# Two of every 64 tiles of both gather sums fetched row by row by SyncE and ScalarE, and copied into the ring by VectorE

## The chip, the core and the metric

The program runs on one NeuronCore of a Trainium2 chip. The metric is the device time of one execution in microseconds (us); lower is better. The core has five engines that run their own instruction streams and meet at semaphores: TensorE (PE), VectorE (DVE), ScalarE (ACT), GpSimd (POOL) and SyncE (SP). Sixteen DMA engines move data between device memory (HBM) and the on-chip memory (SBUF); SP, ACT and POOL can issue DMAs.

## What is computed

Four graph layers over 3,125 nodes of 128 numbers and 100,000 edges. Only the last layer touches the change. Cut to that:

```python
ht = jnp.einsum('ne,reh->rnh', hidden, weights[l])      # 18 transformed rows per node
msg_f = ht[edge_type, src] + biases[l][edge_type]
out = jax.ops.segment_sum(msg_f, dst, num_segments=n_nodes)
msg_b = ht[edge_type + n_rel, dst] + biases[l][edge_type + n_rel]
out = out + jax.ops.segment_sum(msg_b, src, num_segments=n_nodes)
```

So each edge picks one row of 128 numbers (512 bytes) from a table of 28,800 rows, and the rows are summed by node: once forward (table `y_forward`, edges sorted by `dst`) and once backward (table `y_back`, edges sorted by `src`).

## The kernel before

**Tiles, pairs and groups.** The 100,000 sorted edges are 782 tiles of 128 edges (`TILES`), the nodes 25 blocks of 128 (`BLOCKS`). A pair is a tile with a block that its edges fall in; there are 806 pairs. `gather_sum` (L928) works on groups of 8 pairs (`GROUP`), 101 groups in all. It is called twice: with the tag g3 for the forward sum (`back=True`, a straight program without a loop), then g4 for the backward sum (mostly a hardware loop over 8 groups).

**The four streams of a gather sum.** POOL issues one indirect DMA per tile (L1032), which fetches 128 rows into one of 64 slots of the ring `got` (8 groups; `RING` = 8). From tile group 8 on it first waits (L1029) until TensorE has finished group g-5, so it can be five groups ahead. DVE makes, for each group n, the 8 one-hot matrices `hot` in one instruction (`compare`, L1042), at the earliest when TensorE has finished group n-4, four buffers being there. TensorE (`landed_group`, L1124) loads 16 register values (8 column and 8 slot offsets), waits for `hot` and for the eight landings of the group, and multiplies 8 pairs into PSUM.

**What runs beside it in g3.** The table `y_back` for g4 is computed inside g3. Behind every group 15b/4 (rounded down) TensorE multiplies block b in three pieces (`rows_of`, L1139), each of which waits for DVE's bias addition of the piece before; DVE does `bias` for block b (L1046) when its loop is at the group after. The two buffers `y[:, 0]` and `y[:, 1]` are stored by SP (even b) and ACT (odd b) in `keep_rows` (L974), and `bias` of block b waits for the store of block b-2. Also in g3, the index tables of g4 are made: DVE's `climb` at group 3, a table turned by TensorE behind group 6, `locals_of` and `rows_named`, and seven pieces that TensorE flattens (`flatten`, L1148), six of them copied out of PSUM by ACT (L1008). In g4 SP and ACT have no work.

**Order.** All of this order is written by hand: by the place of each call in the loop over n.

Of the kernel before, what the change touches and what calls it, by code (L numbers as in the profile page):

```python
# [71 lines left out]
BANK = 512  # L72

# [854 lines left out]
def gather_sum(nc, S, dram, tag, name, table, index, fresh=True, back=False):  # L928
# [5 lines left out]
    WHOLE, REST = divmod(GROUPS, RING)  # L934
    with ExitStack() as stack:
        m = Memory(nc, stack)
        got = m.sb(tag + "_got", [P, SLOTS * D])
        hot = m.sb(tag + "_hot", [P, WAYS, GROUP, P])
# [6 lines left out]
        if back:  # L945
# [11 lines left out]
                                           "listed", "order", "packed", "built", "flat", "placed", "filed"))  # L957
            by_src = dram["rec_by_src"].rearrange("(t e) r -> t (e r)", e=P)
# [3 lines left out]
            CLIMB_AT, ROWS_AT, FLIP_AT, LOCAL_AT, NAMED_AT, ROWS_BEFORE = 3, 8, 6, 24, 30, 8  # L962
# [11 lines left out]
        def keep_rows(eng, k, first, last):  # L974
            for b in range(first + k, last, 2):
                eng.wait_ge(biased, (b + 1) * PIECES)
                eng.dma_start(dram["y_back"][b * P:(b + 1) * P, :], y[:, k, :]).then_inc(saved[k], 16)
            if last == BLOCKS:
                eng.wait_ge(saved[k], 16 * ((BLOCKS + 1 - k) // 2))

        @block.sync
        def _(sp):
            if back:
                even = TILES // 16 * 16
                sp.dma_start(firsts[0:1, 0:even].rearrange("o (a b) -> o a b", a=16),
                             by_src[0:even, 0:1].rearrange("(a b) o -> o a b", a=16), allow_slow_non_contiguous=True).then_inc(fetched, 16)
                sp.dma_start(firsts[0:1, even:TILES], by_src[even:TILES, 0:1].rearrange("a o -> o a"),
                             allow_slow_non_contiguous=True).then_inc(fetched, 16)
                sp.wait_ge(fetched, 32)
                sp.dma_start(dram["src_firsts"].rearrange("(a n) -> a n", a=1), firsts[:, :]).then_inc(stored, 16)  # L990
                sp.wait_ge(stored, 16)
                sp.dma_start(s.climb[:, :], dram["src_firsts"].rearrange("(a n) -> a n", a=1).to_broadcast([P, TILES])).then_inc(climbing, 16)
                keep_rows(sp, 0, 0, ROWS_BEFORE)
                sp.wait_ge(listed, 1)
                sp.dma_start(S["src_steps"][0:1, :].rearrange("o (c p) -> o c p", p=P), s.turned_columns[:, :]).then_inc(filed, 16)
                sp.wait_ge(built, 1)
                sp.dma_start(tile_rows[:, 0:full, :], by_src[0:full * P, :].rearrange("(c p) r -> p c r", p=P)).then_inc(carried, 16)
                sp.dma_start(tile_rows[0:rest, full, :], by_src[full * P:TILES, :]).then_inc(carried, 16)
                keep_rows(sp, 0, ROWS_BEFORE, BLOCKS)
                sp.wait_ge(filed, 16)  # L1000

        @block.scalar
        def _(act):
            if back:
                keep_rows(act, 1, 0, ROWS_BEFORE)
                for n, (array, k, lo, hi) in enumerate(flats):
                    act.wait_ge(flat, n + 1)
                    act.activation(array[:, lo:hi], free[:, 0:hi - lo], ACT.Copy).then_inc(placed, 1)  # L1008
                keep_rows(act, 1, ROWS_BEFORE, BLOCKS)
                act.wait_ge(placed, len(flats))  # L1010

        @block.gpsimd
        def _(pool):
# [6 lines left out]
            for g in range(TILE_GROUPS):  # L1020
# [10 lines left out]
                for c in range(g * GROUP, min((g + 1) * GROUP, TILES)):  # L1031
                    pool.indirect_dma_start(out=got[:, (c % SLOTS) * D:(c % SLOTS + 1) * D], out_offset=None, in_=table,  # L1032
# [3 lines left out]
        def _(dve):  # L1036
# [38 lines left out]

            def locals_of():
# [4 lines left out]
            def rows_named():  # L1081
# [6 lines left out]
                                         t[:, 0:full, :, 2], ALU.mult, ALU.add).then_inc(built, 1)  # L1088

            if back:  # L1090
                for n in range(GROUPS):
# [14 lines left out]
                dve.wait_ge(built, 2)  # L1106
                dve.wait_ge(listed, 1)
            else:
                with dve.Fori(0, WHOLE) as i:
                    for k in range(RING):  # L1110
                        dve.wait_ge(summed[k % WAYS], i * (RING // WAYS) + (k // WAYS + 1))
                        compare(k % WAYS, start_of(i, k))
# [5 lines left out]
        def _(pe):  # L1118
# [5 lines left out]
            def landed_group(i, k, lands, pairs=GROUP):  # L1124
# [4 lines left out]
                if lands:  # L1129
                    pe.wait_ge(landed[k], i * (16 * GROUP) + 16 * lands)  # L1130
# [914 lines left out]
def norm_and_messages(nc, S, dram):  # L2045
# [4 lines left out]
    with ExitStack() as stack:  # L2050
# [38 lines left out]
        def _(act):  # L2089
# [11 lines left out]
            for b in range(BLOCKS):  # L2101
# [4 lines left out]
                if b == FLAT_AT:  # L2106
                    act.wait_ge(flat, 1)
# [3 lines left out]
            act.wait_ge(placed, 1)  # L2111
# [93 lines left out]
def gnn_kernel(nc, ins, out):  # L2205
# [14 lines left out]
    with ExitStack() as stack:  # L2220
# [54 lines left out]
        with ExitStack() as last:  # L2275
# [3 lines left out]
            S["src_steps"] = r.sb("src_steps", [1, 3 * PAIR_COLS], I32)  # L2279
            with ExitStack() as third:  # L2280
# [5 lines left out]
                gather_sum(nc, S, dram, "g3", "dst", tables[0], S["d_msg"], back=True)  # L2286
            gather_sum(nc, S, dram, "g4", "src", tables[1], S["s_msg"], fresh=False)
# [25 lines left out]
```

## Time and profile before

| | |
|---|---|
| median of 3 runs | 5433.64 us (5424.72 to 5434.58) |
| the profiled execution | 5436.53 us, of which the span is 5434.8 us |
| POOL busy over the span | 3413.0 us (63%), 3213 instructions |
| PE busy over the span | 3062.4 us (56%) |
| g3, first to last indirect DMA | 3150.1 to 4278.8 us |
| g4, first to last indirect DMA | 4292.2 to 5397.8 us |
| TensorE's granted clock | 0.62 of full speed in g3, 0.57 in g4 |

The two gather sums take the span from 3150 to 5411 us, 42% of it; what follows is a short last normalisation. An instruction's row in a timeline gives its start, its duration, its engine, its line, what it writes and reads, how many like it were merged, and in brackets how long the engine was idle before it and which event ended that idle time. "issue" means that the engine waited for nothing that the profile shows. A group of instructions that share a line gives the number, and the shortest, median and longest duration in ns.

### The profile page before, as it was taken

The page shows a single profiled execution, that of the slowest core. Times are in us where ns is not written, and L with a number is a line of the kernel's source. Part 1 is how long each engine was busy: PE and PEld are TensorE (multiplying, and loading weights), DVE is VectorE, ACT ScalarE, POOL GpSimd, SP SyncE. Part 2 cuts the span into 40 slices and gives each one's busy share as a digit, 9 for nine tenths or more (in the row PEclk, how much of TensorE's full clock was granted, in tenths as well). Part 3 has the DMA queues.
Part 4 walks back from the last instruction along what each step waited for, and adds up shares of the span by engine and source line. Part 5 has one row for each costly group of instructions (what it writes and reads, how often), then busy time and mean ns, then how long its engine had stood idle before and what let it go on. Part 6 is the DMA issues. An engine that isn't in the chain of part 4 may idle for free. (4 is left out here: it accounts for less than half of the span.)

```text
span 5434.8 us, 50013 instructions
## 1 busy us (share of the span) xinstructions
PE 3062.4 (56%) x13750; PEld 2237.6 (41%) x13751; DVE 2231.2 (41%) x2709; ACT 614.3 (11%) x1076; POOL 3413.0 (63%) x3213
## 2 busy tenths in 40 slices
PE   3899989567777777744918633343333333333333
PEld 1788879233333333324917422232222323232223
DVE  7999985445555454568901331111111111101112
ACT  0455540000000000004701000000000000000000
POOL 2888868466556555657770356666666666666664
PEclk7999999666666666657958766665665656555555
DMA  5566667144444444425825332222222111111111
GB/s 177 157 181 192 177 198 230 37 131 138 132 133 139 132 135 130 139 87 159 259 62 195 136 100 70 69 64 60 60 59 60 48 46 46 45 46 46 46 46 46
DMA packets 498663, 599.91 MB, mean 110 GB/s; under 512 B 190115, under 2 KB 367441, under 8 KB 496248
## 3 DMA queue, kind: packets, MB, share of 16 engines
q0 software_dynamic: 117856, 246.12, 16.5%
q1 hardware_dynamic: 337751, 229.77, 14.8%
q10 hardware_dynamic: 42944, 122.68, 6.0%
q8 instruction: 51, 0.84, 0.1%
q14 instruction: 61, 0.49, 0.0%
HBM read 406.69 MB, written 204.36 MB: 112 GB/s over the span
## 5 line engine op out<-in xcount | busy, mean ns | idle before, releaser
L720 POOL DMA_INDIRECT rec_by_src<-rec,pos x782 | 1123.3, 1436 | 524.6 <-issue 238.9
L1132 PE MATMUL ps<-g_got,g_hot 128*128 x3224 | 687.5, 367 | 1225.8 <-issue 797.4
L1132 PEld LDWEIGHTS ps<-g_got,g_hot 128*128 128x128 f32 x3224 | 605.7, 272 | 1320.2 <-issue 1318.9
L1592 POOL DMA_INDIRECT sc_kv<-kv,d_src x806 | 761.8, 945 | 533.9 <-DVE sc_kve L1644 260.2
L1032 POOL DMA_INDIRECT g_got<-y_forward,d_msg x782 | 739.3, 945 | 381.8 <-issue 230.1
L1032 POOL DMA_INDIRECT g_got<-y_back,s_msg x782 | 737.8, 943 | 381.2 <-issue 233.5
L805 PE MATMUL ps<-ln_low,ln_hot 128*125 128x256 f32 x2848 | 620.3, 381 | 20.3 <-DVE ln_low L782 16.1
L805 PEld LDWEIGHTS ps<-ln_low,ln_hot 128*125 128x125 f32 x2848 | 535.6, 188 | 104.8 <-issue 24.4
L1043 DVE TENSOR_TENSOR g_hot<-ps,src_loc 128x1024 f32<-128x1024 f32 x101 | 120.6, 1221 | 992.5 <-remote 450.4
L1699 PE MATMUL ps<-w_e,sc_attrT 128*128 128x512 f32 x404 | 320.0, 887 | 246.0 <-ACT sc_attrT L1611 216.3
L1051 DVE TENSOR_TENSOR g_y<-ps,ms_b 128x384 f32<-128x384 f32 x75 | 41.8, 558 | 808.8 <-remote 474.2
L1695 PE MATMUL ps<-q,sc_hotT 128*128 x1616 | 308.5, 352 | 108.0 <-DVE sc_hotT L1637 92.0
L1644 DVE TENSOR_TENSOR sc_kve<-sc_kv,ps 128x1024 f32<-128x1024 f32 x202 | 244.9, 1212 | 239.2 <-DMA win_rows<-rec_by_dst,win_tilei 163.3
L1695 PEld LDWEIGHTS ps<-q,sc_hotT 128*128 128x128 f32 x1616 | 283.2, 262 | 130.2 <-issue 130.2
L1682 PE MATMUL ps<-sc_locr,ones 1*128 1x512 f32 x404 | 312.8, 864 | 10.4 <-issue 10.4
L1637 DVE TENSOR_SCALAR sc_hotT<-ps,part 128x512 f32<-128x512 f32 x202 | 148.0, 747 | 379.5 <-PE ps L1682 196.3
L1145 PE MATMUL ps<-ms_w,ms_xT 128*128 128x384 f32 x150 | 105.9, 800 | 250.0 <-DVE g_y L1051 166.0
L777 DVE TENSOR_TENSOR ln_low<-col,win_lo 128x1024 f32<-128x1024 f32 x178 | 219.7, 1234 | 4.9 <-PE ps L805 2.6
L782 DVE TENSOR_TENSOR ln_low<-ln_low,win_w 128x1024 f32<-128x1024 f32 x178 | 216.1, 1214 | 0.0
L779 DVE TENSOR_TENSOR ln_hot<-col,win_key 128x1000 f32<-128x1000 f32 x178 | 213.8, 1201 | 0.0
L2030 ACT ACTIVATE n_root<-n_var 128x25 f32<-128x25 f32 x1 | 0.2, 225 | 1812.2 <-DVE n_var L2019 1812.2
L828 ACT ACTIVATE ln_out<-ps 125x1024 f32<-125x1024 f32 x160 | 163.7, 1023 | 311.3 <-PE ps L805 294.5
(323 smaller groups left out, 3283.7 us busy)
## 6 DMA issues: line engine op xcount, KB each, us to landing
linked<-ln_out SPq DMA_DIRECT2D x320, 224.0 KB
ve<-sc_kve ACTq DMA_DIRECT2D x202, 256.0 KB
wv_ve<-ve SPq DMA_DIRECT2D x101, 512.0 KB
l_links<-linked SPq DMA_DIRECT2D x25, 800.0 KB
l_links<-linked ACTq DMA_DIRECT2D x25, 800.0 KB
f_links<-linked SPq DMA_DIRECT2D x25, 800.0 KB
f_links<-linked ACTq DMA_DIRECT2D x25, 800.0 KB
attr_pairs<-ln_feats POOLq DMA_DIRECT2D x7, 2048.0 KB
```

The lines of the kernel that those rows point to most:

```text
L720: pool.indirect_dma_start(out=dram["rec_by_src"], out_offset=bass.IndirectOffsetOnAxis(ap=S["pos"][:, c:c + 1], axis=0), in_=S["rec"][:, c ...
L777: dve.tensor_tensor(low[:, q, :, 0:P], S["col"][:, :].unsqueeze(1).to_broadcast([P, GROUP, P]), S["win_lo"][:, cols].unsqueeze(2).to_broad ...
L779: dve.tensor_tensor(hot[:, q], S["col"][:, 0:KEYS].unsqueeze(1).to_broadcast([P, GROUP, KEYS]), S["win_key"][:, cols].unsqueeze(2).to_broa ...
L782: dve.tensor_tensor(low[:, q, :, P:2 * P], low[:, q, :, 0:P], S["win_w"][:, cols].unsqueeze(2).to_broadcast([P, GROUP, P]), ALU.mult).then ...
L805: last = pe.matmul(ps[0:KEYS, bass.ds(slots[j], 2 * P)], hot[:, q, j, :], low[:, q, j, :], start=False, stop=True, skip_group_check=True)
L1032: pool.indirect_dma_start(out=got[:, (c % SLOTS) * D:(c % SLOTS + 1) * D], out_offset=None, in_=table, in_offset=bass.IndirectOffsetOnAxis ...
L1132: last = pe.matmul(ps[:, bass.ds(columns[j], width)], hot[:, q, j, :], got[:, bass.ds(slots[j], width)], start=False, stop=True, skip_grou ...
L1592: pool.indirect_dma_start(out=kv[:, q, j, :], out_offset=None, in_=dram["kv"], in_offset=bass.IndirectOffsetOnAxis(ap=S["d_src"][:, c:c + ...
L1644: dve.tensor_tensor(kve[:, q].rearrange("p a (k d) -> p k a d", d=D), kv[:, q].rearrange("p k (a d) -> p k a d", a=2), feat(q).rearrange(" ...
L1682: pe.matmul(spread_loc(q), S["ones"][0:1, :], locr[0:1, q, :], start=True, stop=True).then_inc(spread[q], 1)
L1695: pe.matmul(qe(q)[:, j * D:(j + 1) * D], hot_t[:, q, j * P:(j + 1) * P], S["q"][:, bass.ds(cols[j], D)], start=True, stop=True)
L1699: pe.matmul(feat(q), attr_t[:, q % 2, :], S["w_e"][:, :], start=True, stop=True).then_inc(product[q], 1)
```

## The change

In every ring of 64 tiles, two tiles are no longer fetched by POOL: the last tile of group 3 is fetched by ACT, the last tile of group 7 by SP (`HELPERS`). That holds for the first 12 rings (`WHOLE`), so for 24 of 782 tiles in each gather sum. A helper loads eight row numbers at a time into registers from a flat index table (`rows`, new: `d_rows` and `s_rows`), and issues one DMA of one row of 512 bytes for each; 128 of them make a tile. The row lands in a buffer of its own, `aside`, which holds two tiles per helper. DVE waits for 128 landings, copies the tile into its slot of the ring and raises `handed` (`hand`); TensorE waits for `handed` in that group beside seven landings instead of eight. A helper starts on tile k+2 when tile k was handed.

In g4 the helpers do only this (`rows_alone`). In g3 (`rows_and_tables`) the stores of `y_back` and SP's three table DMAs stand between quarters of a tile (32 rows). The six flattened pieces are copied by DVE (`place`) instead of ACT, `FLIP_AT` goes from 6 to 5, and `NAMED_AT` from 30 to 36.

```diff
+            def hand(e, h, count):
+                dve.wait_ge(fetched_rows[e][h], count)
+                dve.tensor_copy(got[:, at:at + D], aside[e][:, h * D:(h + 1) * D]).then_inc(handed[e], 1)
...
+    HELPERS = {"act": RING // 2 - 1, "sp": RING - 1}
+    QUARTER = P // 4
...
+        def fetch_rows(eng, e, kind, i, h, lo, hi):
+            p = tile_of(e, h)
+            for at in range(lo, hi, GROUP):
+                _, named = nc.values_load_multi_w_load_instructions(
+                    rows[p:p + 1, bass.ds(i * P + at, GROUP)], engines=[kind], min_val=0, max_val=ROWS * RELATIONS - 1,
...
+                for j in range(GROUP):
+                    eng.dma_start(aside[e][at + j:at + j + 1, h * D:(h + 1) * D],
+                                  table[bass.ds(named[j], 1), :]).then_inc(fetched_rows[e][h], 16)
+
+        def rows_and_tables(eng, e, kind, k):
+            stored = 0
+            for n in range(4 * WHOLE):
+                i, h = divmod(n // 4, 2)
+                while (stored * 2 + k < BLOCKS and (15 * (2 * stored + k)) // 8 + 2 <= n
+                       and (15 * (2 * stored + k)) // 4 + 1 < n // 4 * RING + HELPERS[e]):
+                    keep_rows(eng, k, 2 * stored + k)
+                    stored += 1
...
+                if n % 4 == 0 and n >= 8:
+                    eng.wait_ge(handed[e], n // 4 - 1)
+                fetch_rows(eng, e, kind, i, h, n % 4 * QUARTER, (n % 4 + 1) * QUARTER)
...
+        def rows_alone(eng, e, kind):
+            for h in range(2):
+                fetch_rows(eng, e, kind, 0, h, 0, P)
+            with eng.Fori(1, WHOLE // 2) as i:
+                for h in range(2):
+                    eng.wait_ge(handed[e], i * 2 + (h - 1))
+                    fetch_rows(eng, e, kind, i, h, 0, P)
...
                 for c in range(g * GROUP, min((g + 1) * GROUP, TILES)):
+                    if c in helped:
+                        continue
                     pool.indirect_dma_start(out=got[:, (c % SLOTS) * D:(c % SLOTS + 1) * D], out_offset=None, in_=table,
...
                     compare(q, n * GROUP)
                     if n - 1 in beside:
                         bias(beside[n - 1])
+                    for e in helper_of(n):
+                        k = n // RING
+                        hand(e, k % 2, (k // 2 + 1) * (16 * P))
+                    if n - 1 in flat_at:
+                        place(flat_at[n - 1])
                     if n == CLIMB_AT:
                         climb()
...
                 if lands:
-                    pe.wait_ge(landed[k], i * (16 * GROUP) + 16 * lands)
+                    own = k in HELPERS.values()
+                    pe.wait_ge(landed[k], i * (16 * (GROUP - own)) + 16 * (lands - own))
+                    for e in helper_of(k):
+                        pe.wait_ge(handed[e], i + 1)
```

**ACT in g3.** Before, its whole stream of g3 is six rows: the stores of blocks 1, 3, 5, 7, then the six copies out of PSUM, then the stores of the eight other odd blocks (`g_y` is `y`).

```order
L977 DMA y_back<-g_y 128x1152 x4
L1008 ACTIVATE src_loc<-ps 128x384 x2
L1008 ACTIVATE src_loc<-ps 128x128
L1008 ACTIVATE s_msg<-ps 128x384 x2
L1008 ACTIVATE s_msg<-ps 128x14
L977 DMA y_back<-g_y 128x1152 x8
```

Now the same engine, where it stores block 9, inside the tile for group 35 (L997 is a row's DMA with the register instruction in front of it, L993 the load of eight row numbers, L1032 the store):

```order
L997 ISA
L997 DMA g_aside_act<-y_forward 1x128
L1032 DMA y_back<-g_y 128x1152
L993 TENSOR_LOAD d_rows
L997 ISA
L997 DMA g_aside_act<-y_forward 1x128
```

The store, which waits for block 9's bias additions, now has the first two quarters of the tile ahead of it and the last two, 64 rows, behind it.

**DVE in g3.** Before, from the bias additions of block 9 on (L1051 `bias`, L1043 `compare`):

```order
L1051 TENSOR_TENSOR g_y<-ps,ms_b 128x384 x3
L1043 TENSOR_TENSOR g_hot<-ps,dst_loc 128x1024 x4
L1051 TENSOR_TENSOR g_y<-ps,ms_b 128x384 x3
```

Now, from the same additions on (L1099 `bias`, L1091 `compare`, L1127 `hand`):

```order
L1099 TENSOR_TENSOR g_y<-ps,ms_b 128x384 x3
L1091 TENSOR_TENSOR g_hot<-ps,dst_loc 128x1024
L1127 COPY g_got<-g_aside_act 128x128
L1091 TENSOR_TENSOR g_hot<-ps,dst_loc 128x1024
L1142 SCALAR_TENSOR_TENSOR rec<-src_rows 14x128
```

One compare behind the additions of block 9, DVE now waits for ACT's tile, with all later compares behind that wait.

## Rows read from the trace of the kernel before

**Rows 1.** The page: busy time of each engine.

```profile
PE 3062.4 (56%) x13750; PEld 2237.6 (41%) x13751; DVE 2231.2 (41%) x2709; ACT 614.3 (11%) x1076; POOL 3413.0 (63%) x3213
```

**Rows 2.** Stretches g3 and g4: bounds, length, busy PE PEld DVE ACT POOL, clock, DMA.

```profile
3150.00:4292.00 1142.00, 412.94 (x1777) 307.41 (x1777) 174.75 (x208) 2.42 (x6) 745.92 (x789) 0.62 0.22 62
4292.00:5411.00 1119.00, 376.78 (x1612) 332.63 (x1612) 120.59 (x101) 0.00 (x0) 737.75 (x782) 0.57 0.17 46
```

**Rows 3.** Line 1032: duration ns min/median/max, first and last start in us.

```profile
L1032 POOL DMA_INDIRECT g_got<-y_forward,d_msg x782: 938/944/2419, 3150.1 to 4278.8; - x196
L1032 POOL DMA_INDIRECT g_got<-y_back,s_msg x782: 938/944/961, 4292.2 to 5397.8; - x196
```

**Rows 4.** Timeline of POOL in g4, around one of its stops.

```profile
5363.67 0.94 POOL L1032 DMA_INDIRECT g_got<-y_back,s_msg  x1 [0.30 <-issue]
5364.92 0.94 POOL L1032 DMA_INDIRECT g_got<-y_back,s_msg  x1 [0.30 <-issue]
5371.55 0.94 POOL L1032 DMA_INDIRECT g_got<-y_back,s_msg  x1 [5.69 <-DMA alpha<-mx_turn]
```

**Rows 5.** Timeline of PE over the same stretch.

```profile
5334.77 2.29 PE L1132 MATMUL ps<-g_got,g_hot 128*128 x9 [6.17 <-DMA g_got<-y_back,s_msg]
5339.25 0.37 PE L1132 MATMUL ps<-g_got,g_hot 128*128 x1 [2.19 <-issue]
...
5370.05 3.42 PE L1132 MATMUL ps<-g_got,g_hot 128*128 x12 [0.33 <-issue]
```

**Rows 6.** Timeline of DVE over the same stretch.

```profile
5370.95 2.36 DVE L1043 TENSOR_TENSOR g_hot<-ps,src_loc 128x1024 f32<-128x1024 f32 x2 [14.95 <-DMA alpha<-mx_turn]
```

**Rows 7.** Timeline of SP at the start: DMAs of a single row.

```profile
4.41 0.22 SPq L163 DMA_DIRECT2D raw_src<-in_src_dram  x1
...
6.62 0.31 SPq L163 DMA_DIRECT2D raw_next<-in_dst_dram  x1
```

**Rows 8.** Line 1603: single-row DMAs of 2 KB on SP.

```profile
L1603 SPq DMA_DIRECT2D sc_locr<-loc x202: 242/365/400, 1070.9 to 2335.5; - x101
```

**Rows 9.** Line 839: DMAs of SP at register addresses.

```profile
L839 SPq DMA_DIRECT2D linked<-ln_out x640: 3/323/2560, 164.9 to 783.8; - x160
```

**Rows 10.** Timeline of SP: four of them in a row.

```profile
398.68 1.96 SPq L839 DMA_DIRECT2D linked<-ln_out  x4
```

**Rows 11.** Line 865: SP and ACT issue at the same time.

```profile
L865 SPq DMA_DIRECT2D l_links<-linked x25: 327/328/807, 786.4 to 912.9; - x25
L865 ACTq DMA_DIRECT2D l_links<-linked x25: 361/362/1052, 786.4 to 912.9; - x25
```

**Rows 12.** Timeline of PE in g3: two groups with sixteen registers loaded between.

```profile
3765.12 2.05 PE L1132 MATMUL ps<-g_got,g_hot 128*128 x16 [0.36 <-issue]
3767.64 2.05 PE L1132 MATMUL ps<-g_got,g_hot 128*128 x16 [0.47 <-issue]
```

**Rows 13.** Timeline of DVE: last bias addition of blocks 9, 13, 17, 19, 21.

```profile
3596.53 0.56 DVE L1051 TENSOR_TENSOR g_y<-ps,ms_b 128x384 f32<-128x384 f32 x1 [1.00 <-PE ps L1145]
...
3761.94 0.56 DVE L1051 TENSOR_TENSOR g_y<-ps,ms_b 128x384 f32<-128x384 f32 x1 [1.74 <-PE ps L1145]
...
3923.91 0.56 DVE L1051 TENSOR_TENSOR g_y<-ps,ms_b 128x384 f32<-128x384 f32 x1 [1.01 <-PE ps L1145]
...
4024.63 0.56 DVE L1051 TENSOR_TENSOR g_y<-ps,ms_b 128x384 f32<-128x384 f32 x1 [1.74 <-PE ps L1145]
...
4116.51 0.56 DVE L1051 TENSOR_TENSOR g_y<-ps,ms_b 128x384 f32<-128x384 f32 x1 [1.74 <-issue]
```

**Rows 14.** Stretches of g3 that end where POOL begins groups 40, 56, 72, 80, 88.

```profile
3150.00:3620.00 470.00, 155.54 (x684) 119.22 (x685) 77.84 (x100) 2.42 (x6) 310.01 (x327) 0.62 0.23 66
3620.00:3802.00 182.00, 73.56 (x289) 52.51 (x288) 28.65 (x33) 0.00 (x0) 120.74 (x128) 0.62 0.22 63
3802.00:3983.60 181.60, 65.47 (x296) 47.89 (x295) 25.51 (x29) 0.00 (x0) 120.78 (x128) 0.64 0.21 60
3983.60:4075.60 92.00, 35.23 (x142) 24.78 (x142) 11.36 (x13) 0.00 (x0) 60.40 (x64) 0.61 0.20 59
4075.60:4165.60 90.00, 30.40 (x130) 21.88 (x130) 12.58 (x14) 0.00 (x0) 60.40 (x64) 0.59 0.21 60
```

**Rows 15.** Timeline of DVE at the start of g3: copy, climb, fifth compare.

```profile
3152.30 0.24 DVE L1039 COPY ps<-col 128x128 f32<-128x128 f32 x1
...
3182.99 0.96 DVE L1058 TENSOR_TENSOR src_climb<-src_climb,rec 128x782 f32<-128x782 f32 x1
...
3198.45 1.22 DVE L1043 TENSOR_TENSOR g_hot<-ps,dst_loc 128x1024 f32<-128x1024 f32 x1 [1.20 <-DVE src_columns L1071]
```

More of the change, by code:

```diff
@@ L925, in load_columns, with gather_sum @@
     return values
-def gather_sum(nc, S, dram, tag, name, table, index, fresh=True, back=False):
+def gather_sum(nc, S, dram, tag, name, table, index, rows, fresh=True, back=False):
     width, WAYS = D, 4
@@ L972, in size, with helper_of @@
             return min(GROUP, PAIRS - n * GROUP)
[L974 to L979, printed above, removed]
+        def helper_of(n):
+            return [e for e, k in HELPERS.items() if n < WHOLE * RING and n % RING == k]
@@ new lines, in tile_of @@
+        def tile_of(e, k):
+            return k * SLOTS + HELPERS[e] * GROUP + GROUP - 1
+        helped = {tile_of(e, k) for e in HELPERS for k in range(WHOLE)}
+        def fetch_rows(eng, e, kind, i, h, lo, hi):
[3 more added lines that the diff above has]
+                    rows[p:p + 1, bass.ds(i * P + at, GROUP)], engines=[kind], min_val=0, max_val=ROWS * RELATIONS - 1,
+                    skip_runtime_bounds_check_because="row numbers are node times relations plus type")
+                for j in range(GROUP):
+                    eng.dma_start(aside[e][at + j:at + j + 1, h * D:(h + 1) * D],
+                                  table[bass.ds(named[j], 1), :]).then_inc(fetched_rows[e][h], 16)
@@ L1004, in _ @@
             if back:
[L1005 to L1010, printed above, removed]
+                rows_and_tables(act, "act", mybir.EngineType.Activation, 1)
+            else:
+                rows_alone(act, "act", mybir.EngineType.Activation)
         @block.gpsimd
@@ L1105, in _ @@
                         rows_named()
-                dve.wait_ge(built, 2)
+                dve.wait_ge(copied, 1)
                 dve.wait_ge(listed, 1)
+                dve.wait_ge(placed, len(flats))
             else:
[L1109 to L1112, printed above, removed]
+                with dve.Fori(0, WHOLE // 2) as i:
+                    for k in range(2 * RING):
+                        dve.wait_ge(summed[k % WAYS], i * (2 * RING // WAYS) + (k // WAYS + 1))
+                        compare(k % WAYS, i * (2 * RING * GROUP) + k * GROUP)
+                        for e in helper_of(k):
+                            hand(e, k // RING, (i + 1) * (16 * P))
                 for k in range(REST):
@@ L2110, in _ @@
                     keep_rows(act, b)
-            act.wait_ge(placed, 1)
+            act.wait_ge(placed, 2)
         @block.tensor
```

46 lines of the change are left out of this document (36 added, 10 removed).

## The prediction

> **What bounds the kernel now.** I read the page first. No engine is busy for more than 63% of the span [rows 1], so the share of busy time names no bound, and the two gather sums have to be read alone. Their stretches [rows 2] show POOL with most work, 746 and 738 us of 1142 and 1119, and TensorE at about a third, at a granted clock of about 0.6. The lines then give what one tile costs POOL: 0.944 us, 782 times in each sum [rows 3]. The timeline adds the 0.30 us between two of them that wait for nothing [rows 4], so a tile is 1.25 us, and 782 of them are 976 us. From first to last indirect DMA, g3 takes 1128.7 us and g4 1105.6 [rows 3]. So POOL's own pace is 87% of each sum, and it stands still for about 153 us in g3 and 130 in g4.
>
> The stops decide what a saved tile is worth. In g4 [rows 4] POOL begins a tile at 5364.92 and the next at 5371.55, 5.69 us idle. The event named there lies far back; what comes free then is seen on DVE, which starts its next compare at 5370.95 after 14.95 us idle [rows 6], since it too waits for TensorE. TensorE [rows 5] had begun at 5334.77, after waiting 6.17 us for a landing, at 9 matmuls in 2.29 us, and then sparse ones with gaps of 2.19 us; from 5370.05 it does 12 in 3.42 us. So for some 35 us after it was made to wait, TensorE is slower than POOL, and POOL catches up with it and stops. I counted such stretches: in g4 one about every 6 to 8 groups, in g3 about every 4. Roughly half of POOL's tiles are issued while one is under way. There POOL's end is set by TensorE, not by its own count of tiles.
>
> **What is removed.** 24 tiles of each sum, two per ring, 2 x 1.25 = 2.5 us of 91 us: a ring turned over in (3983.6 - 3620.0) / 4 = 90.9 us [rows 14], of which 64 x 1.25 = 80 is POOL's own. If every saved tile counted, 24 x 1.25 = 30 us would go from each sum. If only those outside the stops count, half, 15 us. I take 15, since the stops belong to TensorE and the change gives TensorE nothing; the bounds are 5 and 30.
>
> **What a helper's tile costs.** No row shows a register-addressed row fetch like this, so I bound the spacing T of two rows. The cheapest single-row DMA is 0.22 to 0.31 us [rows 7], with 2 KB 0.365 [rows 8]. At a register's address SP takes 0.323 us at the median [rows 9], and with its register instructions four stand in 1.96 us: (1.96 - 0.32) / 3 = 0.55 us from start to start [rows 10]. Both queues issue at once without much harm, 0.328 and 0.362 us [rows 11]. To that comes an eighth of a load of eight numbers. TensorE loads sixteen between two groups that start 2.52 us apart [rows 12], so a load is under 1.26 us, and under 0.16 per row. Ends: 0.24 (a bare DMA) and 0.72. The nearest is the 0.55 of [rows 10], in which slightly more register work stands, so I take **T = 0.58 us**, of which 0.1 is the load at most and something less for the register work. A tile is then 128 x 0.58 = 74 us (31 to 92), a quarter 18.6.
>
> **g4.** Each helper has a ring of 91 us for its tile of 74, and two buffers, so tiles lie ready. At the start ACT's first tile is there after 74 + 2 us, while POOL reaches the group that depends on it after 62 x 1.25 = 77 us: nothing lost (0 to 15). A copy on DVE is 0.24 us [rows 15], 24 of them 6 us on an engine busy for 121 of 1119 us [rows 2]: hidden by its waits, and 6 if that cover is gone. g4: **-15** (-30 to +5).
>
> **g3, the start.** DVE waits in group 3 for ACT's first tile, until about 3150 + 76 = 3226. Before, DVE did its climb in that time (3183 to 3198) and the fifth compare at 3198.45 [rows 15]. Behind the wait now stand the climb of 15 us and the compares of groups 4 and on, so compare 4 comes at about 3243, 45 us later. POOL may run five groups ahead, which takes it until about 3230; then it has to wait until TensorE has caught up with groups 3 and 4. TensorE's groups take 2.5 us at its best [rows 12], POOL's 10, so the lag is won back in part: **+10** (0 to 33).
>
> **g3, the stores.** This is the step that decides. Helpers run in order, and a `y_back` store inside a tile waits for bias additions that DVE does only when its loop is at that group. For ACT they fall late: the store of block 9 has 64 rows of the tile for group 35 behind it, yet block 9's last addition starts at 3596.53 [rows 13], one group ahead of the point where DVE needs this tile. The rows take 64 x 0.58 = 37 us; the addition, landing, copy and the group on TensorE some 6 more: group 35 is done at 3596.5 + 43 = 3640. POOL needs it to begin group 40, at 3620.0 [rows 14]: 20 us late. Two rings on, block 13: 3761.9 + 43 = 3805 against 3802.0: 3 late. From block 17 on three quarters, 96 rows or 56 us, stand behind the store: 3923.9 + 62 = 3986 against 3983.6, 2 late; block 19: 4024.6 + 62 = 4086.6 against 4075.6, 11 late; block 21: 4116.5 + 62 = 4178.5 against 4165.6, 13 late. Blocks 11, 15 and 23 fall early enough. Each lateness moves all that follows, biases too, so they add: **+49**. With T = 0.48 the same sum gives 18, with 0.72 some 106. Each such hold makes TensorE wait, and what followed a wait before was a slow stretch; one that falls now where POOL is already late costs the rest of it: **+13** (0 to 60), my least certain term. SP's stores (even blocks) lie early in their tiles; at nothing, with 15 us if one is late. The six pieces that DVE copies in place of ACT, and the two that move by a few groups, are under 3 us on DVE, hidden by its waits; ACT's copies took 2.42 us in all [rows 2].
>
> g3: -15 + 10 + 49 + 13 = **+57**. Both: 57 - 15 = +42 us. The profiled execution took 5436.5 us, 2.9 above the median of three: 5436.5 + 42 - 2.9 = **5476 us**.
>
> **A rule of the skill that speaks against the copy.** The rows of DVE copies in the gather sums show only one to PSUM, 0.24 us [rows 15], at a time when no stop of POOL can be put down to it. The Trainium skill, page "SBUF — State Buffer", section "SBUF: two separate sides", says that GpSimd can't write its DMA descriptors while DVE runs an fp32 copy from SBUF to SBUF, which `hand` is. By it each of the 48 copies would hold POOL for up to its duration: 48 x 0.24 = 12 us, and 5488 for the sum. No run here shows it yet; the 12 us stand in none of the terms above.
>
> **Rivals.**
> 1. *Tiles are ready, POOL's saving counts: faster.* If T is about 0.45 or less, two quarters take 29 us and three 43; then 3596.5 + 35 = 3631 and 4116.5 + 49 = 4165.5, so the holds shrink to 11 us in all. It decides at T near 0.47. g3 then is -15 + 5 + 11 or better, g4 -15 to -30, and if the saved tiles count in full -60 + 10: 5385 to 5422, in the middle **5405**. For it: the bare single-row DMAs of 0.22 to 0.31 [rows 7]. Against it: 0.55 where registers give the address [rows 10].
> 2. *The gain and the holds cancel.* T about 0.5: holds of 24, start 8, against 30 to 35 saved: **5433**.
> 3. *The helpers are the bound.* If a tile takes longer than the 88 us that a ring would now take, both sums run at the helper's pace. At T = 0.75 a tile is 96 us, and 12 rings in each sum lose 96 - 88 = 8, with nothing saved: 2 x 96 = 190, and g3's holds on top: **5650**. It decides at T = 0.69. For it: single DMAs took up to 2.56 us [rows 9]. Against it: that is the maximum, the median is 0.323.
> 4. *The copy holds POOL* (the mechanism that the skill's page names): POOL waits 48 times for 0.24 us beside the forecast, **5488**. It is inside the forecast's range and would be told by a gap behind 1.25 us at the copies.
>
> **How the numbers follow.** Forecast with its holds in g3 (rival 4 in it) 0.52; rival 1 0.26; rival 2 0.14; rival 3 0.08. The forecast's own range: g4 -30 to +5, g3 from -15 + 18 to some +130, so 5440 to 5555. A range for 8 in 10 has to take in the larger part of rival 1: 5395 to 5560; outside are a tenth of the chance below and the helper-bound case above. A measurement of this kernel can tell about 0.2%, 11 us, from no change, so the three chances are faster 0.26, same 0.15, slower 0.59.
>
> **What the profile after would show.** T as the spacing of SP's and ACT's DMAs of one row, 0.58 and, to bear out rival 1, under 0.47. In g4, 758 indirect DMAs from first to last in about 1090 us. In g3, DVE idle for 20 to 50 us ahead of its copies for groups 35, 67, 75 and 83, and there a stop of POOL ahead of groups 40, 72, 80 and 88; at the start a copy near 3226 and the climb behind it. Rings without a late store would turn over faster than 90.9 us. The prediction is wrong if T is far from 0.58, if the copies find their tile landed, or if POOL's stops shrink in g4, which would make a saved tile worth its full 1.25 us.

## The result: slower by 18% where it was timed, and faster by 1% in other runs

| | before | changed |
|---|---|---|
| median (6 runs each) | 5433.01 us | 6399.34 us |
| ratio, 95% interval | | 1.1785 (1.1771 to 1.1798) |
| g3, first to last indirect DMA | 1128.7 us, 782 tiles | 1592.6 us, 758 tiles |
| g4, first to last indirect DMA | 1105.6 us, 782 tiles | 1562.3 us, 758 tiles |

The prediction, 5476 us with a range up to 5560, was wrong: the size was over 20 times too small. The direction came out right by luck, since what made the kernel slower is not what the forecast had added up. The change costs 966 us, about the same in each sum. The stretches of the profile after, in the columns of [rows 2]:

```profile
3138.00:4775.00 1637.00, 356.94 (x1777) 279.54 (x1777) 182.21 (x239) 0.00 (x0) 723.48 (x768) 0.60 0.15 43
4775.00:6385.00 1610.00, 274.98 (x1612) 256.04 (x1612) 125.20 (x126) 0.00 (x0) 715.11 (x758) 0.57 0.12 32
```

POOL's work fell as planned, TensorE's did not grow, and both stretches are some 500 us longer: waiting. The groups of POOL's indirect DMA (duration in ns, first and last start), answering to [rows 3]:

```profile
L1080 POOL DMA_INDIRECT g_got<-y_forward,d_msg x758: 938/944/1992, 3138.9 to 4731.5; - x190
L1080 POOL DMA_INDIRECT g_got<-y_back,s_msg x758: 938/944/961, 4775.0 to 6337.3; - x190
```

One tile costs POOL 0.944 us as before. Where it stands still, from its timeline in g4 and from that of DVE at the same place:

```profile
5132.43 0.94 POOL L1080 DMA_INDIRECT g_got<-y_back,s_msg  x1 [0.30 <-issue]
5177.22 0.94 POOL L1080 DMA_INDIRECT g_got<-y_back,s_msg  x1 [43.84 <-PE ps L1203]
```

```profile
5041.78 0.23 DVE L1127 COPY g_got<-g_aside_act 128x128 f32<-128x128 f32 x1 [86.92 <-DMA g_aside_act<-y_back]
...
5172.28 0.23 DVE L1127 COPY g_got<-g_aside_act 128x128 f32<-128x128 f32 x1 [99.01 <-DMA g_aside_act<-y_back]
```

Once per ring POOL waits 44 us for TensorE, TensorE for DVE's copy, and DVE 99 us for ACT's rows. From one copy of ACT's tile to the next it is 130.5 us, in place of a ring of 91. So the helper is the bound: 128 rows take 131 us, 1.02 us each, where the prediction had 0.58.

That mean is of two very different rates. Line 997, the row fetch (ns shortest/median/longest), in 30 us in which POOL issues without a gap, and in 30 us in which it stands still:

```profile
L997 ACTq DMA_DIRECT2D g_aside_act<-y_back x8: 7/700/710, 5079.0 to 5105.7; - x8
...
L997 ACTq FUSED_REGOPS  x7: 13/700/700, 5079.1 to 5102.9; - x7
...
L997 ACTq MOVE g_aside_act<-y_back x7: 687/700/710, 5079.8 to 5104.3; - x7
```

```profile
L997 ACTq DMA_DIRECT2D g_aside_act<-y_back x57: 234/235/468, 5137.9 to 5167.8; - x57
...
L997 ACTq FUSED_REGOPS  x56: 37/37/37, 5138.4 to 5167.7; - x56
...
L997 ACTq MOVE g_aside_act<-y_back x56: 29/29/29, 5138.4 to 5167.8; - x56
```

With POOL still, ACT sends 57 rows in 30 us, 0.53 us each. Beside POOL it sends 8. Not only the DMAs are slow: a MOVE between registers, 29 ns otherwise, is recorded with 700 ns. A row is three instructions (FUSED_REGOPS, MOVE, DMA), and from start to start each takes 1.40 us, most often 0.70 us until its recorded end and 0.70 us more until the next one starts: 4.2 us per row.

### The profile page after: what moved, and what is told of

The parts are those of the page before. It is cut to its first block and busy times, and to the rows that moved or that the text cites. A ratio compares the mean times of both kernels' runs of the same rounds, so it can differ in the third digit from the quotient of the medians.

```text
span 6407.2 us, 69573 instructions
## 1 busy us (share of the span) xinstructions
PE 2916.0 (46%) x13748; PEld 2139.4 (33%) x13751; DVE 2241.1 (35%) x2764; ACT 613.3 (10%) x1071; POOL 3362.8 (52%) x3165
## 5 line engine op out<-in xcount | busy, mean ns | idle before, releaser
L1203 PE MATMUL ps<-g_got,g_hot 128*128 x3224 | 542.5, 337 | 2347.4 <-DVE g_got L1127 1987.4
L1203 PEld LDWEIGHTS ps<-g_got,g_hot 128*128 128x128 f32 x3224 | 505.4, 246 | 2400.9 <-issue 2400.1
L1080 POOL DMA_INDIRECT g_got<-y_back,s_msg x758 | 715.1, 943 | 890.7 <-PE ps L1203 520.8
L1080 POOL DMA_INDIRECT g_got<-y_forward,d_msg x758 | 716.1, 945 | 868.8 <-PE ps L1203 555.9
L1127 DVE COPY g_got<-g_aside_act 128x128 f32<-128x128 f32 x24 | 5.4, 227 | 1747.3 <-DMA g_aside_act<-y_back 1024.4
L1216 PE MATMUL ps<-ms_w,ms_xT 128*128 128x384 f32 x150 | 92.4, 708 | 269.9 <-DVE g_y L1099 175.3
L1099 DVE TENSOR_TENSOR g_y<-ps,ms_b 128x384 f32<-128x384 f32 x75 | 41.8, 557 | 470.0 <-remote 287.1
L1127 DVE COPY g_got<-g_aside_sp 128x128 f32<-128x128 f32 x24 | 5.6, 234 | 555.4 <-DMA g_aside_sp<-y_back 299.7
```

The costliest lines, as they stand in the source:

```text
L1203: last = pe.matmul(ps[:, bass.ds(columns[j], width)], hot[:, q, j, :], got[:, bass.ds(slots[j], width)], start=False, stop=True, skip_grou ...
```

## Experiments

The theory (A): while POOL issues indirect DMAs back to back, SP and ACT get through one instruction each in about 1.4 us, whichever it is. The rivals: (B) only the row DMAs are slow beside POOL's; (C) a row at a register's address costs 1.0 us, whatever POOL does. What the prediction gave for the saving, the copies and the late stores was tested too.

The table holds what I worked out from the traces, for both gather sums where g4 is not named: mean spacing of two rows in us when POOL is at least eight tiles into a run without a gap, and when it has been still for over 6 us. How the ends of a run are counted moves the means by some 5%.

| run | instructions per row | beside POOL | POOL still |
|---|---|---|---|
| changed kernel, g4 | 3 | 3.78 us (median 4.20) | 0.55, SP 0.53 us |
| e1_const | 1 | 1.28 (median 1.40) | 0.29 |
| e4_act (ACT alone), g4 | 3 | 3.83 (median 3.54) | 0.54 |
| e12_part64 | 3 | 3.61 (median 4.19) | 0.57 |
| e9_after (the 4660 condition, below) | 3 | 0.55 (median 0.39) | none such |

### e1_const: one instruction per row

```diff
-                for j in range(GROUP):
-                    eng.dma_start(aside[e][at + j:at + j + 1, ...], table[bass.ds(named[j], 1), :])
+            for at in range(lo, hi):
+                row = (at * 221 + h * 7) % 28800
+                eng.dma_start(aside[e][at:at + 1, h * D:(h + 1) * D], table[row:row + 1, :])
```

> Each row's DMA has a constant address, so a row is one instruction instead of three and an eighth of a load (it fetches other rows than the reference). Theory A (instructions): while POOL issues back to back, SP and ACT get through one instruction in 1.40 us, whichever it is. Then a row costs 1.4 us there instead of 4.2, about 72 of 128 rows fit beside a ring's 80 us of POOL work instead of some 25, a ring takes about 100 us instead of 131, and the time is 6399 - 24 x 31 = about 5650 us. Theory B (the row DMAs themselves are slow beside POOL's): the spacing beside POOL stays at 4.2 us, only the rows in POOL's long stops get cheaper (0.55 to 0.3 us, some 100 rows, 18 to 25 us per ring), and the time is about 5900 us.

Measured: 5526.54 us against 5430.91, ratio 1.018 (1.014 to 1.021). Beside POOL, ACT's DMAs:

```profile
L993 ACTq DMA_DIRECT2D g_aside_act<-y_back x19: 13/700/722, 4735.3 to 4759.2; - x19
```

19 rows in 24 us: 1.3 us per row in place of 4.2, with the same DMA. It is the instructions that are slow (theory A), not the DMAs (B). The time is below my 5650, since with POOL held less often a ring of 94 us suffices.

### e2_one: what POOL's saving is worth

```diff
+            if lo == 0:
+                eng.dma_start(aside[e][:, h * D:(h + 1) * D], table[0:P, :]).then_inc(fetched_rows[e][h], 16)
```

> Each helped tile comes by one DMA of 128 neighbouring rows at a constant address (other rows than the reference), with the same buffers, copies and semaphores, so the helpers cost next to nothing and what is left is POOL's saving. The prediction's term, 15 us per sum since only tiles outside POOL's stops count: 5433 - 30 = 5403. If every saved tile counts, 2 x 30: 5373. If a copy holds POOL for as long as it takes, 12 us more than either.

Measured: 5364.73 us, ratio 0.987 (0.985 to 0.989), 66 us less. So every saved tile counts, and the 30 us of the prediction are far too few. The rows of g4:

```profile
L1074 POOL DMA_INDIRECT g_got<-y_back,s_msg x758: 942/947/988, 4256.6 to 5329.7; - x190
```

From first to last 1073.1 us for 758 tiles, 1.42 us per tile with the stops; in [rows 3] it is 1105.6 for 782, also 1.42. At that pace with its stops 48 tiles are 68 us; at POOL's bare 1.25 they are 60. The interval, 58 to 81 us, holds both, and so the runs don't tell them apart. The stops (131 us in g4 before, 126 here) did not grow where tiles were saved, as the halved gain of the prediction would have wanted.

### e3_silent: no indirect DMAs beside the helpers

```diff
-                    if c in helped:
+                    if c in helped or (not back and c >= SLOTS):
                         continue
...
-                    pe.wait_ge(landed[k], i * (16 * (GROUP - own)) + 16 * (lands - own))
+                    pe.wait_ge(landed[k], ... if back else 16 * (GROUP - own))
```

> In the backward sum POOL fetches the first 62 tiles and then nothing (the ring's old content is summed again, so the output differs); the helpers' work is unchanged. Theory A, and B too: without POOL's issuing a row takes about 0.55 us all the time, a tile 70 us, and the backward sum falls from 1610 to about 870 us, the whole to about 5660. Rival C (a row at a register's address simply takes 1.0 us on average, whatever POOL does): the backward sum stays at 12 x 128, 1540 us or more.

Measured: 5715.5 us (one run). Stretches that cover each sum:

```profile
3138.00:4775.00 1637.00, 364.43 (x1777) 285.00 (x1777) 184.48 (x241) 0.00 (x0) 725.22 (x771) 0.59 0.16 43
4790.00:5690.00 900.00, 228.95 (x1596) 214.40 (x1596) 120.63 (x121) 0.00 (x0) 45.26 (x48) 0.64 0.02 6
```

g3 is as long as in the changed kernel, g4 fell from 1610 to some 920 us: 24 tiles of rows on two queues in 12 x 74 us. Rival C is out. With POOL silent the helpers keep the spacing that the prediction had taken from [rows 10]. One run alone, but the difference is 690 us.

### e4_act: ACT alone

```diff
-    HELPERS = {"act": RING // 2 - 1, "sp": RING - 1}
+    HELPERS = {"act": RING // 2 - 1}
```

> Only ACT fetches tiles, one per ring; POOL takes SP's tile back. If each engine has its own limit of one instruction in 1.4 us beside POOL, a ring still takes about 131 us, or 1 us more for POOL's tile: about 6400 us. If SP and ACT share what is left of some common supply, ACT's rows come nearly twice as fast beside POOL, and a ring takes about 105 to 115 us: 5800 to 6000 us.

Measured: 6351.57 us (one run). Taking SP's rows away does nothing for ACT's in g4 (3.83 us against 3.78), and little in g3 (some 3.1 against 3.7), where a supply that both share would have nearly doubled their pace. As far as one run can tell, each engine has its own limit.

### e5_copies16 and e14_copies16: do DVE's copies hold POOL?

Sixteen copies per helped tile in g4 in place of one, on top of e2_one:

```diff
+                for j in range(0 if back else 15):
+                    dve.tensor_copy(spare[:, j * D:(j + 1) * D], aside[e][:, h * D:(h + 1) * D])
                 dve.tensor_copy(got[:, at:at + D], aside[e][:, h * D:(h + 1) * D]).then_inc(handed[e], 1)
```

> e2_one (one DMA per helped tile), with 15 further copies of 128x128 from SBUF to SBUF on DVE beside each of the 24 real ones, in the backward sum alone; the forward sum is that of e2_one. If a copy keeps POOL from issuing for as long as it takes, the backward sum gets 24 x 15 x 0.23 = 83 us longer, 5365 + 83 = 5448 us, with POOL's spacing above 1.25 us at the copies. If POOL and DVE don't meet here, 5365 us as e2_one (0.987 of the time before), POOL's spacing at 1.25, and DVE has the time.

Measured: 4600.15 us, but against 4659.90 for the kernel before: ratio 0.987 (0.986 to 0.989). Beside this run, the very kernel before takes 773 us less than it did for the prediction. From here on I tell two conditions apart by what the kernel before takes in them: the 5430 condition (the runs for the prediction, e1 to e4, e12 to e17) and the 4660 condition (e5 to e11 and e18). The expectations speak of two sorts of chips; whether the condition belongs to the chip, to what surrounds it or to the time was not found (one chip number stands beside both, but numbers may repeat between machines). POOL and the additional copies, in the 4660 condition:

```profile
L1075 POOL DMA_INDIRECT g_got<-y_back,s_msg x758: 941/947/960, 3613.5 to 4560.1; - x190
```

```profile
L1123 DVE COPY g_spare<-g_aside_act x180: 206/217/456, 3618.4 to 4475.1; 128x128 f32<-128x128 f32 x180
```

946.6 us for 758 tiles is 1.25 us each: POOL never stands still in this sum, and 360 additional copies of 0.217 us did not hold it once. 59.8 us less than before are 48 x 1.25 = 60. The same kernel in the 5430 condition:

> One DMA per helped tile, with 15 further SBUF copies on DVE beside each real one in the backward sum. It was 0.987 where before takes 4660 us, no different from without them. On a chip on which before takes about 5430: 5365 if copies don't hold POOL, 5448 if they do.

5347.87 us, 0.988 (0.983 to 0.993), where e2_one had 0.987; 83 us more would have been the price of the lock. POOL's indirect DMAs in g4 take 945 ns at the median and come at 1.42 us per tile, as without the additional copies. The Trainium skill, page "SBUF — State Buffer", section "SBUF: two separate sides", says that GpSimd can't write its DMA descriptors while DVE runs an fp32 copy from SBUF to SBUF. These two runs don't agree with it for copies of 128x128: no cost shows in either condition.

### e6_part32, e7_part64, e10, e11, e12, e17: how many rows are free of charge

n rows of each helped tile by register, the others by one DMA:

```diff
+            if lo == 0:
+                eng.dma_start(aside[e][32:P, h * D:(h + 1) * D], table[32:P, :]).then_inc(fetched_rows[e][h], 16)
+            share = 32 * (hi - lo) // P
+            first = 32 * lo // P
-            for at in range(lo, hi, GROUP):
+            for at in range(first, first + share, GROUP):
```

> Of each helped tile 32 rows come row by row at register addresses, the other 96 by one DMA from a constant address (other rows than the reference). Theory A, as a supply of rows: a ring of 91 us has 80 us of POOL's issuing, in which about 25 rows go out, and 11 us of stops at 0.55 us per row, 20 more, so 45 rows are free of charge. 32 fit: the time of e2_one, 5365 +- 15 us. If rows cost POOL or TensorE something in themselves (packets, queues, the shared instruction memory), a quarter of the change's loss against e2_one appears, (6399 - 5365) / 4 = 258 us: about 5620.

> The same with 64 rows. Theory A: 64 - 45 = 19 rows a ring have to be sent while POOL is stopped, 19 x 0.55 = 10 us, less the 2.5 us saved already counted in e2_one: 5365 + 24 x 10 = 5615 us. Half of the loss in proportion, without a threshold, would be 5880.

Both fell into the 4660 condition and tell nothing of the other: 4598.17 us, 0.987 (0.986 to 0.989), and 4600.05, 0.987 (0.985 to 0.989), the same as one DMA per tile. The same once more:

> 64 rows of each helped tile row by row, the others by one DMA from a constant address. Where rows went out at 0.52 us throughout it was 0.987 of before, as for one DMA per tile. If this chip is one on which before takes about 5430 us: a ring has a supply of 45 rows, and 19 more a ring are sent while POOL is stopped, 10 us, so 5365 + 24 x 10 = about 5615 us; in proportion to the rows, without a threshold, it would be 5880.

> The same with 32 rows. On a chip on which before takes about 5430 us: 32 rows are under the 45 that a ring supplies, so 5365 +- 15 us (0.987); in proportion to the rows it would be 5620. On one on which it takes 4660: 0.987 as measured.

0.987 for both (0.986 to 0.989): 4604.20 and 4602.93 us. Then in the 5430 condition:

> 64 rows of each helped tile row by row, the others by one DMA. On a chip on which before takes about 5430 us: threshold theory (45 rows a ring free of charge, 19 more sent while POOL is stopped at 0.55 us): about 5615 us. In proportion to the rows: 5880. On one on which before takes 4660: 0.987.

5648.41 us against 5418.16, 1.043 (1.039 to 1.047): near the 5615 of a threshold, far from the 5880 in proportion. DVE's copies wait there, for over 1300 us in all; POOL's stops are 296 and 250 us instead of 145 and 131.

> 32 rows of each helped tile row by row, the others by one DMA. On a chip on which before takes about 5430: from e12_part64 (5648) and e13_third (two of four tiles of SP late in the backward sum at 43 rows a ring) the supply is some 40 rows a ring, so 32 lie ready: 5365 to 5385. In proportion to the rows, between 5365 and 5648: 5500. On one on which before takes 4660: 0.987.

(All four of SP's tiles were late in the backward sum of e13_third, not two, as written there; of ACT's it was two.) Measured 5393.52 us, 0.996 (0.994 to 0.998): 46 us over e14_copies16, in which no row is fetched singly. In proportion between 0 and 64 rows it would be some 150. The threshold is there, but soft: POOL's stops in g3 are 166 us, with 130 in e14_copies16. Which tiles are late there I didn't follow up.

### e8_third and e13_third: the change at a third of its density

One tile per helper in every third ring (`EVERY = 3`), the stores of `y_back` between pieces of 16 rows. The loops of DVE and TensorE in g4 are rewritten to turn every three rings; of the edit one line:

```diff
-            return k * SLOTS + HELPERS[e] * GROUP + GROUP - 1
+            return (k * EVERY + EVERY - 1) * SLOTS + HELPERS[e] * GROUP + GROUP - 1
```

> The change with one tile per helper in every third ring: 4 tiles each, 8 in each sum, with y_back's stores between pieces of 16 rows. The supply of theory A is 45 rows a ring and engine, 135 in three rings, against 128 needed: the tiles lie ready, and POOL is spared 16 x 1.25 = 20 us over both sums: 5433 - 20 = 5413 us (0.996). If the supply is smaller than 43 rows a ring, DVE waits for the tiles and it is 5440 to 5550.

In the 4660 condition: 4640.56 against 4659.90, 0.996 (0.994 to 0.997), 16 x 1.25 = 20 us less.

> One tile per helper in every third ring. On a chip on which before takes about 5430: 128 rows in three rings are under the supply of 135, so 5410 us (0.996); if the supply is smaller, DVE waits and it is 5440 to 5550. On one on which before takes 4660: 0.996 as measured.

In the 5430 condition: 5452.99 us, 1.007 (1.005 to 1.010). What DVE waited for ahead of its 16 copies:

```profile
  DMA g_aside_sp<-y_back: 136.4, 4
  issue: 49.0, 1
  DMA g_aside_act<-y_back: 34.7, 2
```

SP's four tiles in g4 are all late. 43 rows a ring are a little more than the supply; my 45 was too high.

### e9_after: the changed kernel in the 4660 condition

> The changed kernel itself, beside e10_part64, to see which of two behaviours this chip shows. In the runs e5 to e8 the kernel before took 4660 us, POOL stood still for only 13 us in each gather sum, and rows went out at 0.52 us on average beside it. If this chip is like that: a tile takes 68 us of an 80-us ring, so tiles lie ready in the backward sum, 30 us saved; in the forward sum the late stores (64 and 96 rows behind a bias addition, 34 and 50 us) hold TensorE, some 20 to 60 us, so the ratio to before is 0.99 to 1.005. If POOL's stops are back and before takes about 5430 us, it is 1.178 as at first.

Measured: 4615.51 us against 4663.69, ratio **0.9895 (0.9879 to 0.9912)**. The same two kernels as in the result, and the change gains 48 us. The row fetch in 30 us beside POOL:

```profile
L997 ACTq DMA_DIRECT2D g_aside_act<-y_back x59: 222/222/467, 3999.8 to 4029.9; - x59
L997 ACTq FUSED_REGOPS  x58: 37/37/37, 4000.1 to 4029.8; - x58
```

and POOL in the same stretch (count, busy time and mean, idle time before):

```profile
L1080 POOL DMA_INDIRECT g_got<-y_back,s_msg x24 | 22.7, 946 | 7.3 <-issue 7.3
```

Here the mechanism that I had forecast can be read without the other one. The wait for the first tile, and one for a tile behind a late store, from POOL's timeline:

```profile
2735.58 0.95 POOL L1080 DMA_INDIRECT g_got<-y_forward,d_msg  x1 [0.30 <-issue]
2742.55 0.95 POOL L1080 DMA_INDIRECT g_got<-y_forward,d_msg  x1 [6.02 <-PE ps L1203]
...
3440.92 0.95 POOL L1080 DMA_INDIRECT g_got<-y_forward,d_msg  x1 [0.30 <-issue]
3446.05 0.95 POOL L1080 DMA_INDIRECT g_got<-y_forward,d_msg  x1 [4.19 <-PE ps L1203]
```

and DVE ahead of the second:

```profile
3441.02 0.23 DVE L1127 COPY g_got<-g_aside_act 128x128 f32<-128x128 f32 x1 [50.60 <-DMA g_aside_act<-y_forward]
```

They cost 6 us and 4 us, and with two short ones 12 us in all in g3: the difference between 60 and 48.

### e15_pause and e16_lead3: POOL's gaps, in the kernel before

```diff
+                if g > 0:
+                    if g > 1:
+                        pool.wait_ge(paused, 2 * (g - 1))
+                    for k in range(2):
+                        pool.iota(pad[:, k * TILES:(k + 1) * TILES], ...).then_inc(paused, 1)
```

> The kernel before, with POOL writing two counting rows of 128x782 to a spare place between two groups of 8 tiles, some 1.7 us each time, 170 us per gather sum. On a chip on which before takes about 5430: if issuing without a gap is what brings the instructions of 1.40 us, the pauses keep them away, TensorE has no slow stretches, and POOL's stops of 145 and 131 us go: 5433 + 340 - 275 = about 5500 us. If the slow instructions come whatever the gaps, the pauses add or fill some of the stops: 5600 to 5770, with TensorE's slow stretches still there. On a chip on which it takes 4660: 5000.

In the 5430 condition: 5422.19 us against 5417.57, 1.001 (0.999 to 1.003). 194 pauses, and the time is the same. POOL and TensorE in g4:

```profile
4741.08 3.66 PE L1139 MATMUL ps<-g_got,g_hot 128*128 x16 [7.58 <-DMA g_got<-y_back,s_msg]
...
4749.87 0.95 POOL L1039 DMA_INDIRECT g_got<-y_back,s_msg  x1 [0.30 <-issue]
4750.82 1.55 POOL L1036 IOTA g_pad<- 128x782 f32 x2
4752.53 0.96 POOL L1039 DMA_INDIRECT g_got<-y_back,s_msg  x1 [0.16 <-issue]
```

POOL has no stop left but the pauses (eight tiles, then 2.66 us to the next where 1.25 would be). Of TensorE's slow stretches nothing is left: from 3200 to 5400 us its trace has one spacing within 0.03 us of 0.70 or 1.40, in place of some 660 before. So it is POOL's issuing without a gap, or at more than one tile in 1.43 us, that makes TensorE's instructions slow; which of the two was not separated. My 5500 was still wrong, on the high side: a pause is 1.41 us, not 1.7, and the stops that it replaces are as long.

```diff
-                freed = g - RING + 3
+                freed = g - 3
```

> The kernel before, with POOL three groups ahead of TensorE instead of five. If POOL's stops are the price of TensorE's slow stretches, a shorter lead makes POOL stop earlier, which ends the slow stretch earlier: about the same time, 5400 to 5480 us. If the lead is what covers landing and summing, each slow stretch costs two groups of 10 us more: 5700 or more. On a chip on which before takes 4660: the same as before.

5434.68 us, 1.003 (1.001 to 1.004), with stops of 143 and 141 us. TensorE's slow spacings fell to 107, a sixth, and the time stayed. So did POOL's pace: 1115.7 us for 782 tiles in g4 here, 1105.6 before, 1073.1 for the 758 of e2_one, each 1.41 to 1.43 us per tile. The 1114.5 us with pauses don't bear on this: eight tiles at 1.25 and a pause of 1.41 are 1.43 us per tile by themselves, and that the pauses are just as long as the stops is luck.

One tempting account is that a tile's DMA takes 1.42 us in this condition, so that DMAs queue up behind a POOL that issues in 1.25. The DMA records contradict it. Each tile of g4 is 16 packets of 4096 bytes and 16 of 4 bytes. The last of these ends a median of 2.13 to 2.20 us after POOL's issue, and never more than 3.2, in the kernel before, the changed kernel, e2_one, e14 to e16 (5430 condition) and in e5 and e9 (4660 condition) alike. The tiles do not queue. What holds the other engines' instructions stays open.

A rival that no run tests is the recording itself. e14_copies16 and e5_copies16 are the same kernel in the two conditions. Both traces have all 50,460 records of instructions, but e5 has 16.0 semaphore updates per tile of g4, one for each packet of 4 bytes, and e14 has 2.5; over the whole run it is 78,025 against 33,489. So in the 5430 condition records of updates are lost. A slow instruction there is two steps of 0.70 us, as if its start and its end each waited, and POOL's tiles are what brings most updates. Every execution here, the timed ones too, has a span and a granted clock beside its time, so each seems to have been recorded. Whether the kernels show the slow instructions, or the 5430 us, without recording was not measured.

### e18_after_pause: the pauses in the changed kernel

```diff
+                if g > 0:
+                    for k in range(3):
+                        if 3 * (g - 1) + k:
+                            pool.wait_ge(paused, 3 * (g - 1) + k)
+                        pool.iota(pad[:, :], pattern=[[P, 512]], ...).then_inc(paused, 1)
```

> The changed kernel, with POOL writing three counting rows of 128x512 to a spare place between two groups of 8 tiles, some 1.5 to 1.8 us. On a chip on which before takes about 5430 and e15_pause 5422: if the slow instructions of SP and ACT come from POOL's issuing without a gap, a row takes 0.53 us throughout, a tile 70 us of a ring of 62 x 1.25 + 8 x 1.6 = 90 us, tiles lie ready, and the time is 5422 - 2 x 24 x 1.25 = 5362 us, plus some 12 us for the first tile and late stores in the forward sum: 5375 (0.99). If SP's and ACT's own two streams bring the slow state back, the ring goes back towards 130 us: 5900 to 6400. On a chip on which before takes 4660: rows as in e9_after, the pauses cost 2 x 100 x 1.4 = 280 us, about 4890.

It fell into the 4660 condition, where there is nothing to cure: 4924.80 us, 1.057 (1.056 to 1.059), the price of the pauses. Whether they take away the change's loss in the 5430 condition was not measured and stays open.

## The prediction, step by step

**What bounds the kernel.** Right that POOL's stops decide. Wrong what they are: "the stops belong to TensorE" put the cause at the wrong end. TensorE was slow in these stretches because POOL had issued without a gap, and the row to see it by stood in the trace before. In the timeline of TensorE in g4, kernel before:

```profile
4838.75 0.37 PE L1132 MATMUL ps<-g_got,g_hot 128*128 x1 [2.22 <-issue]
4841.55 0.37 PE L1132 MATMUL ps<-g_got,g_hot 128*128 x1 [2.43 <-issue]
4844.35 0.37 PE L1132 MATMUL ps<-g_got,g_hot 128*128 x1 [2.43 <-issue]
```

A weight load and a matmul in 2.80 us, waiting for nothing shown: 1.40 us per instruction, beside a POOL that issues. I had read it as a slower TensorE. It is the spacing that SP's and ACT's instructions have beside POOL too, and the change put 4800 more instructions per queue and sum just there.

**What is removed.** 15 us per sum was half of what e2_one showed (33); in the 4660 condition it was 30. A saved tile counts in full, whether at 1.25 or at 1.42 us.

**A helper's row: the step that failed.** T = 0.58 us with an upper end of 0.72. Measured some 0.53 with POOL still, and 0.55 beside POOL in the 4660 condition, so the sum of instructions was good; in the 5430 condition 4.2 us beside POOL, a mean of 1.02. With it went the overlap in "Each helper has a ring of 91 us for its tile of 74": the tile took 131 us, the helper became the bound, and 24 rings lost some 40 us each, 966 us in all. The nearest row [rows 10] was nearest in form, not in surroundings. At 398 us POOL does issue beside SP, but DMAs most of which take it twice as long:

```profile
396.42 1.94 POOL L720 DMA_INDIRECT rec_by_src<-rec,pos  x1 [0.30 <-issue]
398.66 1.95 POOL L720 DMA_INDIRECT rec_by_src<-rec,pos  x1 [0.30 <-issue]
400.93 0.97 POOL L720 DMA_INDIRECT rec_by_src<-rec,pos  x1 [0.32 <-issue]
```

Rival 3 named the right bound, a helper slower than the ring, with a chance of 0.08 and a T of 0.75.

**g3, start and stores.** Can't be told apart in the 5430 condition, where both sums lose alike. In the 4660 condition: the first copy at 72 us after the start (forecast 76), POOL late by 6 us (10); the late stores cost 4 us for one and under 3 for the others (49), and nothing of the 13 us for slow stretches behind them shows. The direction was right and the term some seven times too large there: it hung on T (0.48 gave 18, and it was 0.53) and on times of the bias additions that were read from a trace with POOL's stops in it.

**The copies.** Hidden, right; the 12 us of rival 4 did not appear.

## What to carry to other kernels

An instruction on a queue costs what its surroundings allow: before moving work to an idle engine, look in the trace for what the instructions of any engine cost at that very place, above all beside a GpSimd that issues indirect DMAs back to back, and count instructions, not only DMAs. A regular spacing with "issue" behind it (here 1.40 us) is a finding and not a property of the engine that shows it. And a verdict can belong to where and when it was measured, and perhaps to how: these two kernels stand at 1.18 in one condition and at 0.99 in the other, and as far as the runs show, neither was ever timed without being recorded.

## What was unexpected of the hardware

- Two conditions: the kernel before takes 5393 to 5444 us in one, 4652 to 4666 in the other, and nothing between. In the gather sums POOL keeps 1.25 us per tile in the 4660 condition, in the other 1.42 with its stops. That is only part of the difference: in e14_copies16 the first gather sum begins at 3144 us, in e5_copies16, the same kernel, at 2643, so some 500 of the 748 us between the two arise before the change's place is reached. The duration of one indirect DMA on POOL is the same, 0.944 to 0.947 us. What makes the difference was not found.
- In the 5430 condition, an instruction takes 1.40 us from start to start while POOL issues without a gap, on SP, ACT and TensorE alike, a register MOVE as much as a DMA. POOL itself keeps its 1.25 us, and for DVE no row shows it. In g4 it begins some 1 to 9 us into such a run for SP and ACT in the changed kernel, mostly 34 us into it for TensorE in the kernel before where POOL had run for so long, and for SP and ACT ends some 2 to 5 us after POOL has stopped. That 1.40 lies near to the 1.42 us of a tile may be chance; no run shows a link.
- A pause of 1.41 us between eight tiles keeps TensorE's slow instructions away and costs no time in the 5430 condition; in the 4660 condition pauses cost 5.7% (in the changed kernel). For SP and ACT it was not measured, and shorter pauses weren't tried.
